# Reordering the first pass of a macaron Mamba block: where its two u-products and their followers stand in a step

## The reference

```
x = x + 0.5 * ffn(layernorm(x))     # ffn: x @ (ternary W * scale).T + bias
x = x + mamba(layernorm(x))
x = x + 0.5 * ffn(layernorm(x))

mamba(x): u, z = split(x @ W_in.T)
          u    = silu(conv_b + causal 4-tap convolution of u)
          dt_r, B, C = split(u @ W_xproj.T)         # 64, 16, 16 columns
          dt   = softplus(dt_r @ W_dt.T + b_dt)
          h_t  = exp(dt_t * A) * h_(t-1) + dt_t * B_t * u_t
          y    = (h_t . C_t + u * Dskip) * silu(z)
          return y @ W_out.T
```

## Time and profile before

| | |
|---|---|
| median of 3 runs | 3271.41 us (3269.67 to 3273.12) |
| span of the profiled execution | 3268.6 us, 2.8 us under the median |
| TensorE busy | 2496.3 us, 76% |
| VectorE busy | 2817.1 us, 86% |
| ScalarE busy | 1748.4 us, 53% |
| GpSimd busy | 1770.5 us, 54% |

### The profile page before, as it was taken

How to read it: one execution, slowest core, us unless ns; L and a number is a source line. 1 busy time by engine, 2 the same in 40 slices (tenths; PEclk the granted TensorE clock), 3 DMA queues, 4 the chain that set the end, 5 groups by cost and what they waited for, 6 DMA issues and landing times.

```text
span 3268.6 us, 41805 instructions
## 1 busy us (share of the span) xinstructions
PE 2496.3 (76%) x12320; PEld 1443.0 (44%) x12320; DVE 2817.1 (86%) x3588; ACT 1748.4 (53%) x3158; POOL 1770.5 (54%) x1499
## 2 busy tenths in 40 slices
PE   3577988988987366777787777777877777778777
PEld 1233434443433144454454454444544444445444
DVE  5565776776666599999999999999999999999994
ACT  2335675676657655555555555555554555554542
POOL 1111222222211367777777677777776777777773
PEclk8689999999988577988889889888898898898989
DMA  6543323332322522212121121121221221212101
GB/s 213 210 156 118 123 97 111 113 127 90 113 103 78 218 96 68 68 43 72 57 78 68 55 82 69 43 73 56 78 70 55 75 76 43 71 56 78 42 26 39
DMA packets 145153, 286.70 MB, mean 88 GB/s; under 512 B 32448, under 2 KB 81856, under 8 KB 140544
## 3 DMA queue, kind: packets, MB, share of 16 engines
q1 hardware_dynamic: 144896, 283.68, 25.1%
HBM read 174.06 MB, written 109.58 MB: 87 GB/s over the span
## 4 chain that ended last, share of the span: by engine, by line
POOL 25%; issue 23%; DVE 16%; PE 1%; POOLq 1%; DMA 0%; ACT 0%; DVEq 0%; SPq 0%
POOL dbu L1015 19%; DVE h L1185 9%; DVE y L1195 5%; POOL x L1041 2%; POOL o L1047 1%; POOL y L1037 1%; POOL carry L1028 1%; POOL dbu L1021 1%; PE p_g L1320 1%; POOLq L40 1%; DVE tokt L1217 1%; PE p_g L1310 0%; POOL small L69 0%; DVE q L1208 0%; DMA edge_dt<-dt_scratch 0%
## 5 line engine op out<-in xcount | busy, mean ns | idle before, releaser
L1104 ACT ACTIVATE p_da<-dt,neg_a 128x256 f32<-128x256 f32 (+1 forms) x2048 | 892.2, 468 | 934.1 <-DVE h L1185 933.1
L1185 DVE TENSOR_TENSOR_SCAN h<-p_da,carry,dbu 128x512 f32<-128x512 f32 x1024 | 1253.3, 1265 | 20.2 <-POOL dbu L1021 16.0
L1015 POOL TENSOR_TENSOR dbu<-dtu,bb 128x1024 f32<-128x1024 f32 x512 | 1197.2, 2360 | 1.7 <-issue 1.0
L1287 PE MATMUL p_ht<-ident,h 128*128 128x128 f32 x4096 | 658.9, 322 | 378.5 <-DVE h L1185 376.1
L1287 PEld LDWEIGHTS p_ht<-ident,h 128*128 128x128 f32 x4096 | 569.1, 167 | 494.9 <-issue 300.6
L1195 DVE SCALAR_TENSOR_TENSOR y<-p_ht,ct,y 128x1024 f32<-128x1024 f32 x512 | 645.1, 1260 | 0.0
L1320 PE MATMUL p_g<-wo,tokt 128*128 128x512 f16 x1536 | 357.2, 391 | 3.3 <-DVE tokt L1217 3.3
L706 PE MATMUL p_u<-xz,wu 128*128 128x512 f16 x1536 | 350.3, 386 | 0.0
L1329 PE MATMUL p_g<-wz,xz 128*128 128x512 f16 x1536 | 349.4, 385 | 0.0
L1028 POOL TENSOR_TENSOR carry<-h,carry_factor 128x8 f32<-128x8 f32 x254 | 52.3, 206 | 516.2 <-DVE h L1185 514.5
L358 POOL TENSOR_TENSOR late<-dt,u 128x512 f32<-128x512 f32 x64 | 82.4, 1287 | 425.4 <-DVE dt L550 425.4
(11 more groups left out here) (113 smaller groups left out, 2753.0 us busy)
## 6 DMA issues: line engine op xcount, KB each, us to landing
bb<-b_scratch SPq DMA_DIRECT2D x128, 256.0 KB, 3.2
xin<-in_x SPq DMA_DIRECT2D x32, 512.0 KB, 4.3
x_scratch<-x SPq DMA_DIRECT2D x32, 512.0 KB, 3.3
xz_scratch<-xz SPq DMA_DIRECT2D x16, 1024.0 KB, 5.8
y_scratch<-late SPq DMA_DIRECT2D x32, 512.0 KB, 2.9
dt_scratch<-dt SPq DMA_DIRECT2D x64, 256.0 KB, 2.2
dtu_scratch<-late SPq DMA_DIRECT2D x64, 256.0 KB, 2.5
dt<-dt_scratch SPq DMA_DIRECT2D x16, 1024.0 KB, 5.8
```

Of the source, the lines that this page charges most:

```text
L1015: nc.gpsimd.tensor_tensor(state[:, 4 * f:4 * f + 4, :], dtu[par][:, 4 * f:4 * f + 4, :], bb[n // NB % 2][:, n % NB:n % NB + 1, :].to_broad ...
L1104: ins_ = nc.scalar.activation(p_da[p % 2][:, k * T2 + k:(k + 1) * T2], dt[par][:, g, k:], ACT.Exp, scale=neg_a[:, g, n:n + 1])
L1185: nc.vector.tensor_tensor_scan(h[n % 2][:, 2 * p:2 * p + 2, :].rearrange("p g t -> p (g t)"), p_da[p % 2][:], dbu[n % 2][:, 2 * p:2 * p + ...
L1287: mm = nc.tensor.transpose(p_ht[t][:, g * P:(g + 1) * P], h[n % 2][:, g, t * P:(t + 1) * P], ident[:])
```

## The change

TensorE now has s phase 0, turn(0), u product 2j, s phase 1, ffn, s phase 2, u product 2j+1, turn(1), s phase 3. Both products are followed up in their own step: ScalarE has u_work(2j) ahead of s phase 1 and silu(2j) ahead of s phase 2, then u_work(2j+1) behind `normalise(1)`, with silu(2j+1) at the end; s phase 2 stands ahead of `normalise(1)` in every step. VectorE has s phase 0 ahead of the first row statistics, conv(2j) behind `w_work`, and conv(2j+1) *ahead* of the second `low`. ScalarE's `w_high` moves ahead of `normalise(0)`. For the first chunk of the s part, ScalarE and VectorE get waits for the end of the split and its stores (the shared memory). GpSimd's and the DMA queue's lists stay as they are. `had_u` goes.

```diff
--- before.py
+++ after.py
@@ -196,11 +196,6 @@
             v = units.index((kind, g))
             return v % 2, d * NU + v // 2 + 1
 
-        def had_u(i, j):
-
-            before = i if j else i - 1
-            return not isinstance(i, int) or 0 <= before < C1
-
 
         ITEMS, PER_STEP = 24, 3
 
@@ -425,6 +420,10 @@
 
                             wait(act, s_full[v % 2], d * NU + v // 2 + 1)
                             wait(act, dt_done, q - 1)
+                            if isinstance(d, int) and d == 0:
+                                act.wait_ge(w_item_done, ITEMS)
+                                for b in range(2):
+                                    act.wait_ge(parts_stored[b], 16 * 4)
                             nc.scalar.activation(rel[g % 2], p_s[v % 2][:], ACT.Relu, bias=dt_b[:, g:g + 1])
                             nc.scalar.activation(ex[g % 2], p_s[v % 2][:], ACT.Abs, bias=dt_b[:, g:g + 1]
                                                  ).then_inc(s_free[v % 2], 1)
@@ -457,39 +456,37 @@
                 def step(i, par, j, f_on, u_on, s_on):
                     f = i + 1
                     k = f * TT1 + j
-                    before = (i if j else i - 1, (2 * j - 1) % G)
-                    if had_u(i, j):
-                        u_work(*before)
                     if f_on:
                         wait(act, ffn_full, k * 2)
                         for b in range(2):
                             high(0, k, xt[:, 0, 4 * b:4 * b + 4, :], b)
                     if s_on:
                         s_work(i - 1, j, 0)
+                    w_high(i, j)
+                    if u_on:
+                        u_work(i, 2 * j)
+                    if s_on:
                         s_work(i - 1, j, 1)
                     if f_on and not last(k):
                         normalise(0, xin[(j + 1) % 2][:], k + 1)
-                    w_high(i, j)
-                    if had_u(i, j):
-                        silu(before[0], par if j else 1 - par, before[1])
-                    if s_on and j == 0:
+                    if u_on:
+                        silu(i, par, 2 * j)
+                    if s_on:
                         s_work(i - 1, j, 2)
                     if f_on:
                         normalise(1, x1[j % 2][:], k)
                     if u_on:
-                        u_work(i, 2 * j)
+                        u_work(i, 2 * j + 1)
                     if f_on:
                         if j == 0:
                             wait(act, u_full, (f - 1) * G)
                             wait(act, xz_stored[1 - par], (f - (1 - par)) * 16)
                         for b in range(2):
                             high(1, k, xz[1 - par][:, 0, j // 2, 4 * b:4 * b + 4, (j % 2) * P:(j % 2 + 1) * P], b)
-                    if s_on and j:
-                        s_work(i - 1, j, 2)
                     if s_on:
                         s_work(i - 1, j, 3)
                     if u_on:
-                        silu(i, par, 2 * j)
+                        silu(i, par, 2 * j + 1)
 
                 drive(act, step, prologue)
 
@@ -530,6 +527,9 @@
                         if kind == "y":
                             wait(dve, s_full[v % 2], d * NU + v // 2 + 1)
                             wait(dve, y0_stored[g // 2 % 2], (d * 2 + g // 4) * 16)
+                            if isinstance(d, int) and d == 0:
+                                for b in range(2):
+                                    dve.wait_ge(parts_stored[b], 16 * 4)
                             nc.vector.tensor_copy(y0[g // 2 % 2][:, :, (g % 2) * P:(g % 2 + 1) * P],
                                                   p_s[v % 2][:].rearrange("p (t n) -> p t n", t=TT1)).then_inc(s_free[v % 2], 1)
                             if g + 2 < G:
@@ -635,16 +635,16 @@
                     if f_on:
                         for b in range(2):
                             low(0, k, xt[:, 0, 4 * b:4 * b + 4, :], xt[:, 1, 4 * b:4 * b + 4, :], b)
-                    if f_on:
-                        if not last(k):
-                            wait(dve, x_loaded[(j + 1) % 2], (f * 2 + (j + 1) // 2 + 1) * 16)
-                            row_stats(dve, nc, xin[(j + 1) % 2], stats[0], mv[0], vn[0], small[:, 40:41], ln_chain[0],
-                                      stats_ready[0], scale_ready[0], k + 1)
-                    if had_u(i, j):
-                        conv(i if j else i - 1, (2 * j - 1) % G)
+                    if s_on:
+                        s_work(d, 1 - par, j, 0)
+                    if f_on and not last(k):
+                        wait(dve, x_loaded[(j + 1) % 2], (f * 2 + (j + 1) // 2 + 1) * 16)
+                        row_stats(dve, nc, xin[(j + 1) % 2], stats[0], mv[0], vn[0], small[:, 40:41], ln_chain[0],
+                                  stats_ready[0], scale_ready[0], k + 1)
                     w_work(i, j)
-                    if s_on:
-                        s_work(d, 1 - par, j, 0)
+                    if u_on:
+                        conv(i, 2 * j)
+                    if s_on:
                         s_work(d, 1 - par, j, 1)
                     if f_on:
 
@@ -660,12 +660,12 @@
                                   scale_ready[1], k)
                     if s_on:
                         s_work(d, 1 - par, j, 2)
+                    if u_on:
+                        conv(i, 2 * j + 1)
                     if f_on:
                         for b in range(2):
                             hi, lo = (xz[1 - par][:, a, j // 2, 4 * b:4 * b + 4, (j % 2) * P:(j % 2 + 1) * P] for a in range(2))
                             low(1, k, hi, lo, b)
-                    if u_on:
-                        conv(i, 2 * j)
                     if s_on:
                         s_work(d, 1 - par, j, 3)
                     if u_on and j == TT1 - 1:
@@ -746,12 +746,6 @@
                         s_work(i - 1, 1 - par, j, 0)
                     if f_on:
                         turn(0, k)
-                    if s_on:
-                        s_work(i - 1, 1 - par, j, 1)
-                    if f_on:
-                        ffn(k)
-                    if s_on:
-                        s_work(i - 1, 1 - par, j, 2)
                     if u_on:
                         if j == 0:
                             for b in range(2):
@@ -759,12 +753,18 @@
                             if isinstance(i, int) and i == 0:
                                 pe.wait_ge(w_item_done, 8)
                         u_product(i, par, 2 * j)
+                    if s_on:
+                        s_work(i - 1, 1 - par, j, 1)
+                    if f_on:
+                        ffn(k)
+                    if s_on:
+                        s_work(i - 1, 1 - par, j, 2)
+                    if u_on:
+                        u_product(i, par, 2 * j + 1)
                     if f_on:
                         turn(1, k)
                     if s_on:
                         s_work(i - 1, 1 - par, j, 3)
-                    if u_on:
-                        u_product(i, par, 2 * j + 1)
 
                 drive(pe, step, prologue)
 
```

More of the change, by code:

```diff
@@ L637, in step @@
                             low(0, k, xt[:, 0, 4 * b:4 * b + 4, :], xt[:, 1, 4 * b:4 * b + 4, :], b)
-                    if f_on:
-                        if not last(k):
-                            wait(dve, x_loaded[(j + 1) % 2], (f * 2 + (j + 1) // 2 + 1) * 16)
-                            row_stats(dve, nc, xin[(j + 1) % 2], stats[0], mv[0], vn[0], small[:, 40:41], ln_chain[0],
-                                      stats_ready[0], scale_ready[0], k + 1)
-                    if had_u(i, j):
-                        conv(i if j else i - 1, (2 * j - 1) % G)
-                    w_work(i, j)
                     if s_on:
                         s_work(d, 1 - par, j, 0)
+                    if f_on and not last(k):
+                        wait(dve, x_loaded[(j + 1) % 2], (f * 2 + (j + 1) // 2 + 1) * 16)
+                        row_stats(dve, nc, xin[(j + 1) % 2], stats[0], mv[0], vn[0], small[:, 40:41], ln_chain[0],
+                                  stats_ready[0], scale_ready[0], k + 1)
+                    w_work(i, j)
+                    if u_on:
+                        conv(i, 2 * j)
+                    if s_on:
                         s_work(d, 1 - par, j, 1)
@@ L748, in step @@
                         turn(0, k)
+                    if u_on:
+                        if j == 0:
+                            for b in range(2):
+                                wait(pe, tr_split[b], (i * TT1 + TT1) * 2)
+                            if isinstance(i, int) and i == 0:
+                                pe.wait_ge(w_item_done, 8)
+                        u_product(i, par, 2 * j)
                     if s_on:
@@ L755, in step @@
                     if u_on:
-                        if j == 0:
-                            for b in range(2):
-                                wait(pe, tr_split[b], (i * TT1 + TT1) * 2)
```

(4 more changed lines are left out.)

## The result

The change makes the kernel slower: median 3284.71 us of 4 runs (3284.25 to 3287.35) against 3271.0 of 4 (3269.67 to 3273.12), a ratio of 1.0043 with a 95% interval of [1.0028, 1.0057]. The forecast was 3260.6, faster; the result lies 1.7 us above the upper end of the range. The profiled execution took 3284.39 us, with a span of 3282.6 and a mean granted clock of 0.873 (before 0.883).

The account below looks back on a forecast made before the run. TensorE was taken as the fullest engine, with some 14 us of holes a round, closely coupled to the others. Full rounds +3.5, round 0 -12.3, rounds 7 and 8 -2: -10.8, so 3260.6 us, range 3243 to 3283.

Parts of the forecast that it names:

- the full round: Each of rounds 1 to 6, all three parts running: 116.1 us against 116.2 before; six rounds 696, so +3.5 us.
- the walk: Pricing a full round by following its four steps through the coupled engines: 112.9 us, before any charge for the clock.
- step 1: Full round, turn(0) to turn(0): softplus ahead of normalise(1) puts turn(1) at 20.6, plus 4.2: 24.8 us.
- Round 0: Round without s part: shorter turn(1) to turn(0), less conv(0) and half clock, plus w_high's 1.7 us: -12.3 us.
- Rounds 7 and 8: Last rounds of the first pass: x unit's silu comes earlier, ScalarE's softplus stays the bound: -2 us.
- The price of the lost cover: After turn(1), no product covers the chain: next turn(0) 4.2 us later (4.6 in step 0), y0 8.3 us later.
- rival 3: Slower: at the round's end, the clock costs 6.6 us, not 3.2; a round takes 119.5, the kernel 3281; chance 0.19.
- the charge for the clock: Half clock behind idle stretches, per full round: 1.9 behind y0, 0.8 and 0.5 at tails of steps 0 and 2.
- step 0: Full round, y0 to next turn(0): TensorE sets the time up to turn(1), then 4.6 us: 30.8 us.
- step 2: Full round: VectorE's late FFN eviction gives turn(1) at 23.0, 3.2 late for TensorE, plus 4.2: 27.2 us.
- step 3: Full round: ScalarE is full, turn(1) comes at 21.8, plus 8.3 to y0: 30.1 us.
- round -1: w_high ahead of normalise(0) moves only what next waits behind normalise(1); priced at nothing.

Follow-up runs that it names:

- its experiment: Kernel before, with only ScalarE's w_high moved ahead of s work and normalise(0): 3262.95 us, ratio 0.9977.
- filling that hole alone: Changed kernel plus 28 matmuls with unused product (about 6.1 us) in TensorE's idle stretch ahead of y0, rounds 1 to 6: 3268.61 us, ratio 0.9994.
- after: The kernel with the whole change, against the kernel before: 3284.71 us, ratio 1.0043.
- one of 1.89 us: Changed kernel plus 8 matmuls with unused product in the idle stretch ahead of y0: 3288.09 us, ratio 1.0048.
- all holes filled: Changed kernel plus unused matmuls: 28 ahead of y0, 9 ahead of turn(0) in step 1, 5, 13, 5 ahead of turn(1) in steps 1 to 3: 3257.73 us.
- The fastest kernel: Changed kernel with times_dskip for group 0 ahead of conv(7), second low ahead of conv(2j+1), silu(2j+1) behind the next step's first high: 3230.17 us.

## Why the prediction was wrong

In short: the term that failed is the full round, put at 116.1 us, 112.9 from the walk and 3.2 for the clock. It took 120.9, some 115.6 without the half clock and 5.3 for it.

**Right.** ffn waits no more; y0 waits 6.7 to 6.8 us for `times_dskip` (6 to 7 forecast); y0 starts 8.32 behind turn(1) (8.3). turn(0) follows turn(1) after 4.49, 4.55 and 4.12 us (4.6, 4.2, 4.2), waiting 2.07 for `low` at the start of step 1; the 4.55 is not `low`, as forecast, but the second d unit, which waits 0.77 for its bank (667.28). turn(1) waits 1.08, 2.99 and 1.09 in steps 1 to 3 (0.8, 3.2, 0.8). Round 0: -11.55 against -12.3, though `w_high` has a larger part in it than the 1.7 us I gave: 8.6 less 5.1, so 3.5, in its experiment. With that the other terms of round 0 came to some 8 and not 10.6, so that its sum was in part luck. Rounds 7 and 8: +1.6 and -2.8, so -1.2 against -2. The price of the lost cover was seen, and rival 3 named the place, though it gave the whole excess to the clock.

**Wrong, first: the charge for the clock, 3.2 us a round.** It is 5.3 on average, from 120.9 less 115.6. I charged 1.9 behind y0: the turn 0.9 and the product "the rest". The rows above show turn 0.9, product 1.7 and y0 0.45 more, about 3; filling that hole alone gave 2.7 back. The tail of step 0 was charged 0.8, where turn and product are 1.75 us longer together (641.09, 642.86); that of step 1, with holes of only 1.08 and 0.77 us, was charged nothing and costs as much (668.33, 670.08). The tail of step 2 was charged 0.5: turn(1) behind its hole is 0.9 longer (692.95), and in three of the six rounds turn(0) and the product of step 3 are longer too, by 0.9 and 1.45 (817.30, 819.07). The first three places make 6.5 us of longer rows in the round shown, some of it taken up by the waits that follow: the round itself is 4.5 us above 115.6, the mean of the six 5.3. I scaled the length of the slow stretch by the earlier trace rows, where the hole was 2.8 us and no product stands behind the turn: there y1 and ffn follow, and ffn runs at full clock (611.64, 7.08 us for 32 matmuls). The Trainium skill (TensorE: Matmul & The Clock Gate, The HAM clock gate) has the throttled clock as the default; the fillings agree, 0.91 to 0.99 with nothing else changed. The direction was in the prediction, the size was not.

**Wrong, second: the walk, 112.9 us.** With the clock restored the round takes 115.6. By steps, from that kernel's rows and forecast: step 0 30.5 (30.8), step 1 25.7 (24.8), step 2 28.7 (27.2), step 3 30.7 (30.1). The largest miss is step 2, where turn(1) comes 24.6 after turn(0) and not 23.0. VectorE and GpSimd of after in order of time show where it begins:

```profile
673.25 2.35 POOL L364 TENSOR_TENSOR x<-xin,half_bias 128x1024 f32<-128x1024 f32 x1
...
674.78 1.11 DVE L541 TENSOR_SCALAR res<-late 128x512 f32<-128x512 f32 x1
...
680.71 2.58 DVE L512 SCALAR_TENSOR_TENSOR acc<-up,conv_w,acc 128x512 f32<-128x512 f32 x2
...
681.47 1.27 POOL L353 TENSOR_TENSOR late<-dt,u 128x512 f32<-128x512 f32 x1
...
684.99 0.42 DVE L541 TENSOR_SCALAR res<-late 128x512 f32<-128x512 f32 x1
```

The same L541 takes 1.11 us where it begins during GpSimd's addition and 0.42 without it, and two taps take 2.58 where the second begins during the product of dt and u, 1.54 at 720.61 without one. My prices were of the undisturbed kind: in rounds 1 to 8 of the kernel before, no L541 took over 0.43 us and no tap over 0.75. These two, 0.7 and 1.0, would make the 1.6 us; that is read from the trace and was not tested by itself. Steps 1 and 3 lie 0.9 and 0.6 over the walk. In step 1 some 0.35 is the d unit's wait for its bank that the walk left out; no run says what the rest is.

The two terms make the miss of the six rounds: 6 x 2.1 for the clock and 6 x 2.7 for the walk are 28.8, where 725.55 less the forecast 696 is 29.6.

**Wrong, third: round -1 "moves only what next waits".** It gained 4.8 us. VectorE's remainder of a weight item and turn(1) of the step, after:

```profile
86.82 4.61 DVE L628 SCALAR_TENSOR_TENSOR wu<-u,tmp,wu 128x2048 f16<-128x2048 f32 x2
...
98.98 1.57 PEld L685 LDWEIGHTS p_tr<-ident,xn 128*128 128x128 f32 x8 [6.10 <-ACT xn L388]
```

and before:

```profile
88.11 1.24 ACT L393 ACTIVATE xn<-xin,small 128x1024 f32<-128x1024 f32 x1 [3.35 <-POOL small L71]
...
91.28 4.61 DVE L628 SCALAR_TENSOR_TENSOR wu<-u,tmp,wu 128x2048 f16<-128x2048 f32 x2 [4.10 <-ACT wu L454]
...
103.44 1.57 PEld L685 LDWEIGHTS p_tr<-ident,xn 128*128 128x128 f32 x8 [9.84 <-ACT xn L393]
```

ScalarE's `w_high` (84.39 after) stood behind a normalise that itself waited 3.35 us for GpSimd's scale, VectorE waited 4.10 us for it, and VectorE's later work, with it turn(1), came 4.5 us later. The wait was in the trace and I had read it only in round 0.

In sum: forecast -10.8, measured +15.4 up to x of round 8. The full rounds miss by 29.6 one way, round -1 by 4.8 the other, the rest by 1.5.

**What moved, then.** A step has three gaps on TensorE that need a cover: turn(0) to ffn, ffn to turn(1), turn(1) to the next turn(0). Two products cover two of them. Before, the first gap was open, and cost 30 us in 14 waits; the change opened the third, which at a round's end held 8.3 us of VectorE work. The first product moved alone opened the second, the dearest (3305.45). Moving one `times_dskip` made the third short enough to leave open, and then the new order beats the old (3239.28 against 3247.94).

## What to carry to other kernels

A block of matmuls that is moved to cover one wait uncovers another: list the gaps of a step with the chain that runs in each, and leave open the shortest, after shortening it. An idle stretch ahead of work that TensorE bounds is to be priced as the stretch plus the slower matmuls behind it, here 6.7 us and some 3 more; short holes that follow each other count too (1.08 and 0.77 us, 1.8 more); and if a hole can't be closed, what ends its chain is the first thing to look at (one operation of 0.5 us moved here was worth 45 us). Split a many-engine reordering into its edits, since one of them may carry the gain (`w_high`, 8 us) and another the loss.

## What the hardware showed that I had not expected

- The half level of the clock outlasts the turn: 24 matmuls take 7.05, 6.80, 6.2 and 5.34 us behind idle stretches of 6.7, 5.0, 2.1 and 0.65. The stretch just ahead does not decide it alone: with `times_dskip` early, 2.15 us of idle time are followed by a product at full clock (702.42, 703.50), and behind 1.08 and 0.77 in after it is slow. A filling of 6 us restored the full level, one of 1.89 us with 4.96 idle behind it did not.
- A VectorE operation that begins while a GpSimd addition or product of whole tiles runs can be held until that one ends. In the rows above L541 ends 0.29 us after the addition (675.89 and 675.60), the second tap 0.55 us after the product (683.29 and 682.74). So the price, here 0.7 and 1.0 us, is the rest of the GpSimd operation and not a fixed factor: of the 56 L541 and the 112 taps of L512 in the full rounds and the two behind them, six each are met so. The FFN eviction L654, which reads one tile from SBUF and one from PSUM, begins during such an operation 15 times and keeps its 0.74 to 0.75 us. The Trainium skill (GPSIMD Engine Reference, section 1, Specifications) has the two engines share SBUF interfaces, with contention where a VectorE instruction has two SBUF inputs or is in a performance mode that uses two ports. L512 has two SBUF inputs: the trace agrees, and adds the size. L541 with one takes only 0.42 us undisturbed, which would fit the second kind; no run here shows its mode.
- In the one round that is longer than its neighbours, TensorE stands idle with no releaser that the profile shows. In the kernel with all holes filled:

```profile
600.06 0.59 PE L727 MATMUL p_s<-ident,ud 128*128 128x128 f32 x2 [1.92 <-issue]
...
602.15 5.88 PE L706 MATMUL p_u<-xz,wu 128*128 128x512 f16 x24
```

That round takes 120.7 us and not 115.6: 1.92 for the hole and the rest mostly for the half clock behind it. The fastest kernel has one of 3.4 us in its round of 115.8, 1.9 of it behind the end of `times_dskip`. Both stand at y0 of round 4. Rounds 2 to 5 are written as a loop of two rounds that runs twice (`Fori` in `drive`), and this y0 is the first work behind the jump back; from 585 to 605 us the trace of the first has five packets of instruction loading, from 540 to 580 two. A delay in loading the code would fit, but no run tests it, and the kernel with one filling has the same jump and the same five packets without such a hole: what it is stays open.
